# Labels two batches ahead, the mask term as a twelfth label column from ScalarE, and row and label sums moved to the scores of a graph-attention kernel

## The reference, cut to what matters

```python
row_zero = exp_v.sum(-1) == 0
q_exp = jnp.where(row_zero[..., None], 0.0, q[:, None, :])
self_feat = concat([exp_v, q_exp], -1) @ W_self.T + b_self
output = self_feat
for d in range(2):
    A = (adj_f if d == 0 else swapaxes(adj_f, 1, 2))[:, :, :20, :]
    cond = A.sum(-1)                      # edges at all?
    vb = A @ w_bias + b_bias              # label bias, 11 labels
    aff = where(cond > 0, qh . kh / sqrt(dh), -9e15) + vb
    output += (softmax(aff) @ kv) @ Wout + bout
return exp_v + relu(output)
```

## Time and profile before

| | |
|---|---|
| runs | 726.74, 730.37, 729.32 us, median 729.32 |
| profiled execution | 726.0 us, span 724.3 us |
| PE busy | 654.3 us (90%) |
| DVE busy | 551.3 us (76%) |
| POOL busy | 441.0 us (61%) |
| ACT busy | 364.6 us (50%) |
| mean granted TensorE clock | 0.970 of full |
| HBM traffic | 107.64 MB, mean 149 GB/s |

### The profile page before, as it was taken

One profiled execution on the slowest core, in us unless ns is written; L12 is line 12 of the kernel. 1 busy time (PEld: TensorE's weight loads), 2 busy tenths in 40 slices (PEclk: granted clock), 3 DMA queues, 4 the chain that ended last, 5 costly groups with the idle time before them and its releaser, 6 DMA issues.

```text
span 724.3 us, 11613 instructions
## 1 busy us (share of the span) xinstructions
PE 654.3 (90%) x3792; PEld 569.6 (79%) x3792; DVE 551.3 (76%) x756; ACT 364.6 (50%) x654; POOL 441.0 (61%) x408
## 2 busy tenths in 40 slices
PE   6989897999979997999989997999889997999975
PEld 6858695987869795987779795988689795979773
DVE  4955657779877888778877888688878887789753
ACT  2616352745465463745465554747283645646413
POOL 0031458655868477755867486855866585866953
PEclk9999999999999999999999999999999999999996
DMA  8934663644746374644645283825645373726051
GB/s 325 398 107 99 111 195 107 139 156 89 224 98 196 93 185 147 166 143 82 242 88 193 70 233 96 227 81 115 217 96 177 83 233 92 219 79 154 6 126 58
DMA packets 54225, 107.64 MB, mean 149 GB/s; under 512 B 27008, under 2 KB 38528, under 8 KB 47488
## 3 DMA queue, kind: packets, MB, share of 16 engines
q1 hardware_dynamic: 52048, 91.70, 40.3%
q0 software_dynamic: 2160, 15.73, 12.0%
HBM read 86.63 MB, written 20.78 MB: 148 GB/s over the span
## 4 chain that ended last, share of the span: by engine, by line
PE 37%; DVE 22%; issue 17%; POOL 13%; ACT 6%; DMA 1%; DVEq 1%; SPq 1%; POOLq 0%; ACTq 0%
PE aff L440 16%; PE aff L422 6%; POOL z L895 4%; POOL xl L876 4%; DVE sff L659 4%; DVE wtl L673 3%; DVE bx L683 3%; PE gen L393 3%; PE gen L394 3%; PE gen L395 3%; POOL z L907 2%; ACT wth L543 2%; DVE rsum L647 2%; DMA wkT<-in_wkT 1%; DVE sff L678 1%
## 5 line engine op out<-in xcount | busy, mean ns | idle before, releaser
L440 PE MATMUL aff<-gh,sfh 128*128 128x320 f32 x512 | 118.9, 314 | 2.2 <-DVE rcp L812 2.2
L440 PE MATMUL aff<-gl,sfh 128*128 128x320 f32 x512 | 117.9, 312 | 0.0
L876 POOL TENSOR_TENSOR xl<-x,xh 128x512 fp32r<-128x512 f32 x64 | 85.2, 1375 | 53.5 <-ACT xh L519 53.5
L440 PE MATMUL aff<-gh,sfl 128*128 128x320 f32 x512 | 117.2, 310 | 0.0
L528 ACT ACTIVATE sfh<-sff 128x512 fp32r<-128x512 f32 x64 | 40.2, 629 | 146.5 <-DVE sff L659 146.5
L393 PE MATMUL gen<-xh,w1h 128*128 128x512 f32 x256 | 107.9, 421 | 0.0
L883 POOL TENSOR_TENSOR z<-cb,bx 128x640 f32<-128x640 f32 x64 | 98.6, 1575 | 12.8 <-PE tp L395 12.8
L880 POOL TENSOR_TENSOR sfl<-sff,sfh 128x512 fp32r<-128x512 f32 x48 | 61.3, 1285 | 67.3 <-ACT sfh L528 67.3
L394 PE MATMUL gen<-xl,w1h 128*128 128x512 f32 x256 | 101.3, 396 | 0.0
L395 PE MATMUL gen<-xh,w1l 128*128 128x512 f32 x256 | 101.0, 395 | 0.0
L619 ACT ACTIVATE z<-z 128x640 f32<-128x640 f32 x64 | 47.2, 738 | 99.7 <-POOL z L895 99.7
(11 more groups left out here) (97 smaller groups left out, 1253.5 us busy)
## 6 DMA issues: line engine op xcount, KB each, us to landing
x<-in_x SPq DMA_DIRECT2D x16, 1024.0 KB, 8.1
xn<-in_xn SPq DMA_DIRECT2D x30, 512.0 KB, 4.1
sff<-in_x POOLq DMA_DIRECT2D x15, 1024.0 KB, 8.2
out_y<-sff SPq DMA_DIRECT2D x15, 1024.0 KB, 4.5
msk<-in_mask SPq DMA_DIRECT2D x16, 880.0 KB, 4.7
cb<-c_scratch SPq DMA_DIRECT2D x16, 320.0 KB, 6.0
nz<-nz_scratch SPq DMA_DIRECT2D x16, 256.0 KB, 3.9
wkT<-in_wkT SPq DMA_DIRECT2D x1, 2048.0 KB, 10.8
```

The lines of the kernel that those rows point to most:

```text
L440: mm = nc.tensor.matmul(aff[:, t % 2, half, 0:SH], s, g[:, f, slot, half * SH:(half + 1) * SH], start=(f == 0 and i == 0), stop=(f == FC - ...
L876: nc.gpsimd.tensor_tensor(xl[:, c, :], x[:, c, :], xh[:, c, :].bitcast(F32), ALU.subtract).then_inc(s_xl, 1)
```

## The change

The labels of batch b + 2 (not b + 1) are worked on during batch b; the prologue does those of batches 0 and 1. ACT makes the mask term in three small activations (`edge_terms`): relu of the mask sum, relu of 1 minus that, and that times -9e15 plus the constant label bias, written as column 11 of `prod`. `label_sum` then adds 12 columns and gives the finished bias; `label_bias` and the threshold go. On DVE `label_sum` and the first `row_sums` move to the head of the batch, the mask sum between the first two shifts, the second `row_sums` and `nonzero` ahead of `add_query` 0, `sf_low` back behind `add_sf` 1. `nonzero` becomes a comparison times a tile of ones. On SP the loads follow: mask three ahead, rows in another order. `scores` waits for the low features block by block. `rcp` takes the place of `ssum`. The host pads rows and mask by a copy of the last batch. Core of the diff (the loop of SP, and the functions):

```diff
-        prod = sb("prod", [P, T, D * M, L])
+        prod = sb("prod", [P, T, D * M, L + 1])
...
@@ SP, prologue
             load_x(0)
+            load_mask(0)
             load_rows(1, 0)
-            load_mask(0)
...
             sp.wait_ge(s_rsum, 3)
             load_rows(1, 1)
+            sp.wait_ge(s_neg, 3)
+            load_mask(1)
 
             for c, (r, nr) in enumerate(v_chunks):
...
-            sp.wait_ge(s_mk, 1)
-            load_mask(1)
             sp.wait_ge(s_xl, FC)
             load_x(1)
...
             store_nonzero(1)
+            load_rows(2, 0)
             sp.wait_ge(s_sfq, FC)
             load_nonzero(1)
+            sp.wait_ge(s_neg, 6)
+            load_mask(2)
@@ SP, batch
                 if ahead == 2:
-                    sp.wait_ge(s_rsum, b * 2 + 4)
-                    load_rows(b + 2, 0)
+                    sp.wait_ge(s_rsum, b * 2 + 5)
+                    load_rows(b + 2, 1)
...
-                    load_x(b + 2)
-                    sp.wait_ge(s_rsum, b * 2 + 5)
-                    load_rows(b + 2, 1)
-                    sp.wait_ge(s_mk, b + 2)
-                    load_mask(b + 2)
+                    sp.dma_start(x[:]..., a["x"]...).then_inc(s_xin, 16)
+                    sp.wait_ge(s_neg, b * 3 + 9)
+                    load_mask(b + 3)
                     store_nonzero(b + 2)
+                    load_rows(b + 3, 0)
@@ PE, scores
-                pe.wait_ge(s_sfl, b * FL + FL)
-                pe.wait_ge(s_sfl2, b * (FC - FL) + (FC - FL))
...
+                        if t == 0 and f < FC - FL:
+                            pe.wait_ge(s_sfl2, b * (FC - FL) + (f + 1))
+                        elif t == 0:
+                            pe.wait_ge(s_sfl, b * FL + FL)
@@ ACT
+            def edge_terms(n):
+                act.wait_ge(s_cond, n + 1)
+                nc.scalar.activation(cond[:], cond[:], ACT.Relu).then_inc(s_neg, 1)
+                act.wait_ge(s_neg, n * 3 + 1)
+                nc.scalar.activation(cond[:], cond[:], ACT.Relu, scale=-1.0, bias=one[:, 0:1]).then_inc(s_neg, 1)
+                act.wait_ge(s_neg, n * 3 + 2)
+                nc.scalar.activation(prod[:, :, :, L], cond[:], ACT.Identity, scale=NEG, bias=wb[:, L:L + 1]).then_inc(s_neg, 1)
...
                 labels(0, range(g, L, LG))
+            edge_terms(0)
...
             evict_g(0, 4)
+            act.wait_ge(s_mskin, 32)
+            act.wait_ge(s_vred, D)
+            labels(1, range(0, L, LG))
+            labels(1, range(1, L, LG))
             sf_high(0, 0, 3)
             for u in range(5, GU):
                 evict_g(0, u)
+            labels(1, range(2, L, LG))
+            edge_terms(1)
...
+                if ahead == 2:
+                    act.wait_ge(s_mskin, b * 16 + 48)
+                    act.wait_ge(s_vred, b * D + 2 * D)
+                    labels(b + 2, range(0, L, LG))
                 for t in range(T):
...
+                    if ahead == 2 and t + 1 < LG:
+                        labels(b + 2, range(t + 1, L, LG))
+                    if ahead == 2 and t + 1 == LG:
+                        edge_terms(b + 2)
@@ DVE
-                nc.vector.tensor_scalar(nzc[:], rsum[:], 0.0, None, ALU.not_equal).then_inc(s_nzc, 1)
+                nc.vector.scalar_tensor_tensor(nzc[:], rsum[:], 0.0, one[:], ALU.not_equal, ALU.mult).then_inc(s_nzc, 1)
...
             g_low(0, 7)
+            label_mask(1)
 
             dve.wait_ge(s_bo, 2)
             nc.vector.memset(rcp[:, 0, 0:1], 0.0).then_inc(s_u, U0)
@@ DVE, batch
                 if ahead >= 1:
-                    label_mask(n)
+                    dve.wait_ge(s_bx, b * T + T)
+                    label_sum(n, 0)
+                    label_sum(n, 1)
+                if ahead == 2:
+                    row_sums(b + 2, 0, xn[:], s_xnin, b * 32 + 48)
                 shift(b, slot, 0)
+                if ahead == 2:
+                    label_mask(b + 2)
                 shift(b, slot, 1)
...
                 if next_g:
                     g_low(i + 1, 0)
+                    total(b, slot, 3)
+                if ahead == 2:
+                    row_sums(b + 2, 1, xn[:], s_xnin, b * 32 + 64)
+                    nonzero(b + 2, True)
                 if ahead >= 1:
                     dve.wait_ge(s_out[other], (i + slot) * 16 + 16)
                     add_query(n, other, 0)
-                total(b, slot, 3)
                 if next_g:
                     g_low(i + 1, 1)
                     g_low(i + 1, 2)
-                if ahead == 2:
-                    row_sums(b + 2, 0, xn[:], s_xnin, b * 32 + 48)
+                else:
+                    total(b, slot, 3)
                 if ahead >= 1:
                     add_query(n, other, 1)
-                    label_sum(n, 0)
...
-                    label_sum(n, 1)
-                    label_bias(n)
                     add_query(n, other, 2)
...
                     g_low(i + 1, 6)
-                if ahead == 2:
-                    row_sums(b + 2, 1, xn[:], s_xnin, b * 32 + 64)
-                if next_g:
                     g_low(i + 1, 7)
-                if ahead == 2:
-                    nonzero(b + 2, True)
...
                 wt_low(b, slot, 2)
-                if ahead >= 1:
-                    sf_low(n, other)
                 wt_low(b, slot, 3)
                 add_sf(b, slot, 0)
                 wt_low(b, slot, 4)
-                for j in range(1, HG):
+                add_sf(b, slot, 1)
+                if ahead >= 1:
+                    sf_low(n, other)
+                for j in range(2, HG):
                     add_sf(b, slot, j)
```

More of the change, by code:

```diff
@@ L78, in build @@
         msk = sb("msk", [P, T, D, M, L], I32)
-        prod = sb("prod", [P, T, D * M, L])
+        prod = sb("prod", [P, T, D * M, L + 1])
         bx = sb("bx", [P, T, D, M])
-        neg = sb("neg", [P, T, D, M])
+        cond = sb("cond", [P, T, D * M])
+        one = sb("one", [P, T])
         cb = sb("cb", [P, S])
@@ L173, in build @@
                                         sem("relu_done"), sem("x_added"), sem("out_done"))
-        s_prod, s_vred, s_cond, s_neg, s_mk, s_bx = (sem("label_prod"), sem("label_sum"), sem("cond_done"),
-                                                     sem("neg_done"), sem("label_bias_done"), sem("bias_done"))
+        s_prod, s_vred, s_cond, s_neg, s_bx = (sem("label_prod"), sem("label_sum"), sem("cond_done"),
+                                                     sem("edge_terms_done"), sem("bias_done"))
         block = ctx.enter_context(nc.Block())
@@ L619, in batch @@
                     nc.scalar.activation(z[slot][:, t, :], z[slot][:, t, :], ACT.Exp).then_inc(s_exp, 1)
-                    if ahead >= 1 and t + 1 < LG:
-                        labels(n, range(t + 1, L, LG))
+                    if ahead == 2 and t + 1 < LG:
+                        labels(b + 2, range(t + 1, L, LG))
+                    if ahead == 2 and t + 1 == LG:
+                        edge_terms(b + 2)
                 for f in range(FC - 1):
@@ L682, in label_sum @@
                     dve.wait_ge(s_prod, n * LG + LG)
+                    dve.wait_ge(s_neg, n * 3 + 3)
                 nc.vector.tensor_reduce(bx[:, :, d, :], prod[:, :, d * M:(d + 1) * M], AX_X, ALU.add).then_inc(s_vred, 1)
@@ L686, in label_mask @@
                 dve.wait_ge(s_mskin, n * 16 + 16)
[L687 to L694, removed]
+                nc.vector.tensor_reduce(cond[:].rearrange("p t (d m) -> p t d m", d=D), msk[:], AX_X, ALU.add).then_inc(s_cond, 1)
             def shift(b, slot, t):
@@ L705, in total @@
                 dve.wait_ge(s_exp, b * T + (t + 1))
[L706 removed]
+                nc.vector.tensor_reduce(rcp[:, t, :], z[slot][:, t, :].rearrange("p (g m) -> p g m", m=M), AX_X, ALU.add).then_inc(s_sum, 1)
                 dve.wait_ge(s_sum, b * T + (t + 1))
[L708 removed]
+                nc.vector.reciprocal(rcp[:, t, :], rcp[:, t, :]).then_inc(s_rcp, 1)
             def value_low(c, d):
@@ L732, in _ @@
             nc.vector.memset(ones_r[:].bitcast(F32), 1.0).then_inc(s_onesr, 1)
+            nc.vector.memset(one[:], 1.0).then_inc(s_one, 1)
             nc.vector.memset(bd[:], 0.0).then_inc(s_zero, 1)
@@ L794, in _ @@
             label_sum(0, 0)
+            label_sum(0, 1)
             add_query(0, 0, 2)
             g_low(0, 2)
-            label_sum(0, 1)
-            label_bias(0)
             value_low(2, 0)
@@ L927, in _ @@
             sf_low(0, 0, 1)
-            pool.wait_ge(s_mk, 1)
+            pool.wait_ge(s_vred, D)
             pool.wait_ge(s_cin, 16)
@@ L960, in batch @@
                         sf_low(n, other, f)
-                    pool.wait_ge(s_mk, n + 1)
+                    pool.wait_ge(s_vred, n * D + D)
                     pool.wait_ge(s_cin, n * 16 + 16)
@@ L990 @@
     ins["x"] = np.ascontiguousarray(x.reshape(B, N, FC, P).transpose(0, 3, 2, 1))
-    ins["xn"] = np.ascontiguousarray(x.reshape(B, P, T, F))
```

(3 more changed lines are left out.)

10 lines of the change are left out of this document (3 added, 7 removed).

## The result

The changed kernel takes 734.3 us (median of 20 runs) against 729.3 for the kernel before (20 runs): ratio 1.0063, 95% interval 1.0037 to 1.0090, that is 4.6 us more, 2.7 to 6.6. The ratio leaves out the two slowest runs of the changed kernel (741.9 and 740.9 us), which count as a slow state, and takes the other 18. The forecast was 729, no change. It is slower, by little, and the interval excludes the forecast.

The account below looks back on a forecast made before the run. TensorE was taken as the bound, with DVE mattering only where TensorE waits for it. Terms -50.3 + 6.9 + 23.1 + 8.4 + 1.0 + 10.7 = -0.2 us, set against the median, gave 729 us, range 705 to 744.

Parts of the forecast that it names:

- the prologue: Before the first scores: stores held for edge terms +6.8, labels +1.9, mask sum +2.0; together +10.7 us, bounds 4 and 14.
- the clock's net effect: Half-clock stretches behind the tail waits go, -11.2 us; new ones behind longer waits add 8.4 (odd) and 1.0 (even).
- what goes: Tail of the batches: transposes' wait -35.0, value products' wait -4.1, seven half-clock stretches -11.2; together -50.3 us.
- the odd batch: Key product 3 waits 3.3 us since total, row sum and test precede `add_query` 0; seven times, +23.1 us.
- the reading by which every odd batch gets one: TensorE's clock follows recent busyness, so every odd batch would have a half-clock stretch: +10.5 us for the +8.4 taken.
- the even batch: Third feature block waits 1.15 us for `add_query` 0 behind late rows, row sum and test; six batches, +6.9 us.
- rival C: Slower: late rows in the even batch decide, wait 2.9 us and clock down; 744 with half the batches hit; chance 0.23.
- some 7.2 a pair: The -50.3 us of removed waits and half-clock stretches, stated as a saving for each pair of batches.
- the first has no store ahead: Even batches: the row wait of 1.15 us counted in six, the first excepted because no store precedes its row load.
- the offset: From the profiled run's 726.0 us to the median 729.3: 3.3 us added to the forecast.
- B: Faster: odd wait 2.8 us without half-clock stretch, rows in time, no even-batch cost; 709 us, chance 0.33.
- D: Tail waits stay because transposes wait for ScalarE's eviction behind `sf_high` 3, not row sums; 761 us, chance 0.03.

Follow-up runs that it names:

- e7: Changed kernel with e1, e3 and e4 together, and labels and mask sum of batch 1 put behind what releases the first scores: 689.6 us.
- e2: Changed kernel, odd batches only: second row sum and test behind `g_low` 1 and 2, fourth total left ahead of `add_query` 0: 716.9 us.
- e3: Changed kernel, odd batches only: fourth total back behind `add_query` 0, second row sum and test behind `g_low` 1 and 2: 706.8 us.
- e12: Changed kernel, unchanged, profiled a second time: 732.4 us.
- e1: Changed kernel with SP issuing the mask of batch 1 behind the first chunk's value stores, not ahead of them: 727.7 us.
- e4: Changed kernel, even batches only: second row sum and test behind `add_query` 0 and the fourth total: 724.4 us.
- e5: Changed kernel with DVE's `sf_low` back ahead of `wt_low` 3, as in the kernel before: 737.2 us.
- e8: Changed kernel with ten unused filler products (2.3 us) on TensorE in odd batches ahead of the wait of key product 3: 727.8 us.
- e9: Changed kernel with e1, e3 and e4 together, labels and mask sum of batch 1 left where the change has them: 690.1 us.
- e11: Kernel before, unchanged, profiled a second time: 731.1 us.
- e10: As e9, with the row load of batch 2 issued ahead of the value loads of batch 0 instead of behind them: 687.9 us.
- b1: Kernel before, with each batch's second row sum and the non-zero test in the loop replaced by tiny memsets: 695.9 us.

## Why the prediction was wrong, by its own steps

In the six later pairs and in the prologue the waits came out where the prediction put them. What failed is the sum made from them, in two terms: the first pair of batches, counted like the other six, and the clock's net effect, put at -1.8 us.

**Right: what goes.** The wait of the transposes fell by 32 us where 35.0 was put, the 4.1 us of the value products went, and no half-clock stretch follows the transposes. What the transposes still wait is 0.2 us at a time. With every cost in the batches taken back (e7) the six pairs are 6.8 us shorter each than in the kernel before, for the 7.2 put.

**Right: the odd batch.** Key product 3 waits 2.8 us, forecast 3.3, bounds 2.4 to 4.4. e2 and e3 show its parts. With its clock it cost 27.6 us (e3) for 23.1 + 8.4 = 31.5 put. The test took 0.56 us there for 0.5, the fourth exp came 1.1 us later than the earlier trace rows has it (+18.7 for +17.6). A stretch followed in 0.6 of the cases (17 of 28 in the profiles after, e12, e1 and e4) where 0.8 was put; the reading by which every odd batch gets one (+10.5) is not borne out.

**Right: the even batch.** The third block waits 0.73 to 1.85 us, forecast 1.15 (to 2.33 in e12). e4 gave back 10.0 us for the 6.9 + 1.0 put (the 1.0 is a slip for 6 x 0.2 = 1.2). 9.0 us of the 10.0 stand in the profiles without any half-clock stretch in an even batch. Nor is there a length "from about 2 us on" that brings the clock down, as rival C had it: waits of 1.79 (e3), 1.81 (e5) and 2.23 us (e1) have a half-clock stretch beside them, waits of 2.20 (e8), 2.33 (e12) and 2.50 us (e2) have none.

**Right within its bounds: the prologue.** From the row load to the first scores it is 11.4 us longer on the mean of the two profiles of each kernel, forecast 10.7. SP's hold of the stores was put at 6.8 and measured as 6.6 us in time and 7.9 in the profile (e1). That the labels and the mask sum cost the prologue 3.9 was right too (4.2 in e7 and e9), but nearly all of it comes back in the first batch.

**Wrong: the sum took seven pairs as alike.** "some 7.2 a pair" was taken off all seven, and "the first has no store ahead" made its row wait nothing. So the first pair should have become 2.7 us shorter (-7.2 + 3.3 + 1.2). In the first profiles it is 0.6 shorter, in the second ones (e11, e12) 1.8 longer, on the mean 3.3 us over the forecast. In this pair it is the even batch that lasts longer than the others: 36.6 and 37.8 us for 33.5 and 33.8. Length, PE busy and granted clock of it in the two profiles, and PE's wait in the second:

```profile
102.62:139.24 36.62, 35.14 (x188) 30.30 (x189) 25.01 (x34) 18.72 (x36) 26.10 (x24) 0.92 0.46 150
...
105.85:143.64 37.79, 34.36 (x188) 29.23 (x189) 25.02 (x34) 18.71 (x36) 26.13 (x24) 0.95 0.48 146
...
116.48 0.57 PE L446 MATMUL aff<-gh,sfh 128*128 128x320 f32 x2 [1.67 <-DVE z L719]
```

The rows of batch 2 are loaded at the end of the prologue behind the value loads, ahead of the first shift of that batch, and DVE waits 3.59 us for them, then 1.01 us for the mask (5.03 and 0.73 in e12). In e12 this reaches PE: it waits 2.2 us for `shift`. In the first profile it reaches PE as 0.24 us only. There a half-clock stretch runs 6.1 us into the batch, and the whole excess is in PE's busy time, 35.14 for 32.06. So the two causes, late rows and a batch that begins at half clock, can hide one another. The kernel before begins at half clock as well, for 3.4 and 5.2 us, so the clock is no cost of the change by itself. How much of the 3.3 us the rows cost stays open: e10, which loads them earlier, is shorter by 2.2 us with overlapping intervals.

On the mean of the two profiles of each kernel the sum runs: -0.2 forecast, +0.7 in the prologue behind the row load, +3.3 in the first pair, -1.6 in the six pairs, -0.6 in the even tail batch that was put at nothing, +0.2 in the last, and -0.2 ahead of the row load, which the change doesn't touch: +1.6 us.

**Wrong: the clock.** Its term was made for the odd and even batches alone, -11.2 + 8.4 + 1.0 = -1.8 us net. PE's wait at 78.69 in the prologue was 6.30 us long, where the kernel before had none there, and a half-clock stretch lies around it with 6.1 us of busy PE in it (3.4 in e12). "One more half-clock stretch" stood in the prologue's bound and not in its value. Over all runs whose clock is on record the time at half clock, worked out from each run's mean clock and span, is 56.9 us in the changed kernel and 50.0 in the kernel before (18 and 51 runs); within each kernel a microsecond more of it goes with 0.43 to 0.46 us more time. That is about 3 us more, for the 1.8 less of the forecast, and it is an estimate from runs that differ by chance, not an experiment; e8 alone shows for the odd batches that the clock costs time. The four profiled executions don't have this difference (50.8 and 48.2 us at half clock against 43.5 and 58.4), which is why they show +1.6 and the runs +4.6.

**And the offset.** The forecast added 3.3 us from profiled run to median. For the changed kernel it is 6.5: its profiled execution was the shortest of all. Spans of 726.1 and 730.7 against 724.3 and 729.4 say +1.3 to +1.8, the runs say +2.7 to +6.6.

**Luck.** The terms had errors of both signs: the odd batch was put 3.9 us too high, the even one 2.1 too low. A forecast of exactly no change was within 5 us of the result partly for that reason.

**The rivals.** B (709, chance 0.33) had the odd wait right at 2.8 us. It failed mainly since the clock did come down behind some of these waits (6.5 us, e8) and the even batches' rows were late (10.0 us, e4), both of which it put at 0. C named the right sign, but the late rows in the even batch weren't what decided: the largest cost is the odd batch's (27.6 against 10.0 us). D fell with b1.

**Open.** Where in the unprofiled executions the extra half-clock stretches lie. The profiles have 4 and 3 of them in the loop, e1's has 5 behind key products, one of them 6.8 us long, and one in an even batch; e8 says about four in a median run's odd batches.

## What to carry to other kernels

A piece of work that moves from a waiting tail to an earlier place takes its cost along if anything there has a margin smaller than the piece: here 0.4 us of margin at a half bank of PSUM, against three pieces of 1.2, 1.2 and 0.5 us. Before moving something ahead of an instruction, write down who waits for that instruction through the other engines; the same removal with another place for the pieces, and for a few loads of the prologue, is some 42 us faster than the kernel before (e10), not 5 slower. Sum the prologue and the first round by themselves, measured from a step that the change doesn't touch, since what lies ahead of it may differ by more than the effect.

## What the runs showed of the hardware that was not expected

A DVE tensor_tensor with both inputs in SBUF (`sf_low`) took 0.68 us while GpSimd was idle, up to 1.14 in the kernel before and 2.13 in e5, with GpSimd in instructions of some 1.6 us beside it; there it made PE 1.3 us late. It isn't held every time: in one even batch of e5 it took 0.68 us amid the same instructions. The new test, with two tensor inputs of four elements, took 0.16 to 0.61 us and in the odd batch ended at 400.37, GpSimd's multiply at 400.35:

```profile
399.29 1.06 POOL L929 TENSOR_TENSOR z<-z,rcp 128x512 f32<-128x512 f32 x1
```

The Trainium skill (SBUF, State Buffer, section "Who interferes with whom") says that a DVE instruction with two SBUF inputs contends with a GpSimd one that reads SBUF. The trace agrees, and adds how long it can last here, up to 1.45 us on top of 0.68.

A wait of 2.8 us amid dense products was followed by a stretch at 0.50 in some odd batches and not in others of one execution (4, 3, 5 and 5 of 7 in four profiles), one of 2.33 us in 2 of 7 (e5), one of 1.24 us in none of seven (e2). Filling 2.3 of the 2.8 us with unused products kept the clock at 1.00 in all seven odd batches and gained 6.5 us.
